# A four-layer graph kernel on one core: the first stage with adjacency products ahead and its loop term on VectorE

## The reference, cut to what matters

```python
# layer 0
msg_in   = (adj   @ x + bias_in ) * sigmoid(x @ gate_w_in  + gate_b_in )
msg_out  = (adj   @ x + bias_out) * sigmoid(x @ gate_w_out + gate_b_out)
msg_loop = x * sigmoid(x @ loop_gate)
y = layernorm(relu(msg_in + msg_out + msg_loop) + x)
# layer 1, its first half
A = adj + I;  dinv = rsqrt(rowsum + colsum - diagonal of A);  A_hat = dinv A dinv
h = relu(batchnorm((A_hat @ y) @ W1.T))          # statistics over all graphs
```

## Time and profile before

| what | value |
|---|---|
| median of 3 runs | 675.87 us (675.26 to 676.02) |
| the profiled execution, its own time | 676.43 us |
| its span in the trace | 674.3 us |
| TensorE busy, matmul / weight load | 634.5 us (94%) / 437.9 us (65%) |
| VectorE busy | 476.5 us (71%) |
| ScalarE busy | 429.0 us (64%) |
| GpSimd busy | 245.8 us (36%) |
| granted TensorE clock, mean | 0.991 of full speed |

### The profile page before, as it was taken

The page is one execution under the profiler, slowest core; times in us unless marked ns, Lnnn a source line. Parts: engine busy times, 40 slices in busy tenths (PEclk is TensorE's granted clock), DMA queues, the critical chain, the costliest instruction groups (busy, mean ns, idle before and its releaser), DMA issues.

```text
span 674.3 us, 9326 instructions
## 1 busy us (share of the span) xinstructions
PE 634.5 (94%) x2698; PEld 437.9 (65%) x2698; DVE 476.5 (71%) x1566; ACT 429.0 (64%) x955; POOL 245.8 (36%) x262
## 2 busy tenths in 40 slices
PE   8899989997799999999999999999999999999993
PEld 6655746545685587577657756765785686577573
DVE  4988886677886757876886787688758766465355
ACT  2766866774946675676668576666847666547562
POOL 4698983003654032324505332431433243002031
PEclk9989999999999999999999999999999999999997
DMA  9224100000000000000000000000000000000000
GB/s 341 95 81 157 44 1 0 1 0 1 0 1 1 0 1 2 0 1 32 1 1 1 32 1 1 32 1 0 2 31 1 0 33 1 0 2 32 1 28 35
DMA packets 4227, 16.83 MB, mean 25 GB/s; under 512 B 464, under 2 KB 464, under 8 KB 4048
## 3 DMA queue, kind: packets, MB, share of 16 engines
q1 hardware_dynamic: 4176, 16.23, 6.3%
HBM read 12.03 MB, written 4.19 MB: 24 GB/s over the span
## 4 chain that ended last, share of the span: by engine, by line
PE 59%; DVE 13%; ACT 7%; issue 3%; POOL 1%; DVEq 0%; ACTq 0%; POOLq 0%
PE QQ L795 21%; PE QQ L807 14%; PE QQ L646 4%; PE PA L750 4%; PE PA L778 3%; PE PB L769 2%; DVE HB L1387 2%; DVE HT L1472 2%; ACT HB L1024 2%; ACT raw L1061 2%; DVE raw L1494 1%; PE PB L731 1%; ACT raw L1073 1%; PE PB L817 1%; PE PA L731 1%
## 5 line engine op out<-in xcount | busy, mean ns | idle before, releaser
L1061 ACT ACTIVATE raw<-QQ,BL 128x256 f32<-128x256 f32 (+4 forms) x312 | 166.8, 558 | 95.6 <-PE QQ L807 52.0
L795 PE MATMUL QQ<-HT,WT 128*128 128x256 f32 (+2 forms) x624 | 205.5, 473 | 6.3 <-ACT raw L1061 3.4
L795 PEld LDWEIGHTS QQ<-HT,WT 128*128 128x128 f32 x624 | 115.8, 190 | 73.1 <-issue 32.1
L396 POOL TENSOR_TENSOR RSD<-VAR,pw 128x8 f32<-128x8 f32 (+1 forms) x42 | 61.8, 1470 | 230.1 <-DVE VAR L1246 230.1
L807 PE MATMUL QQ<-HB,WT 128*128 128x256 f32 (+2 forms) x384 | 114.5, 441 | 1.7 <-DVE HB L1512 1.4
L807 PEld LDWEIGHTS QQ<-HB,WT 128*128 128x128 f32 x384 | 70.1, 190 | 35.9 <-issue 15.3
L510 POOL TENSOR_TENSOR HB<-HB 128x512 f32<-128x512 f32 x28 | 35.2, 1276 | 132.4 <-ACT HB L1014 132.4
L1073 ACT ACTIVATE raw<-raw 128x256 f32<-128x256 f32 (+4 forms) x88 | 41.5, 472 | 39.7 <-DVE raw L1494 31.5
L1484 DVE SCALAR_TENSOR_TENSOR raw<-raw 128x512 f32<-128x512 f32 (+2 forms) x66 | 39.1, 593 | 30.7 <-ACT raw L1061 30.0
L917 ACT ACTIVATE X<-Z,OFF,RSD 128x128 f32<-128x128 f32 x88 | 35.1, 482 | 8.7 <-POOL OFF L402 8.7
L1512 DVE SCALAR_TENSOR_TENSOR HB<-raw 128x256 f32<-128x256 f32 (+4 forms) x48 | 21.9, 457 | 23.2 <-ACT raw L1073 23.2
(11 more groups left out here) (216 smaller groups left out, 1127.4 us busy)
## 6 DMA issues: line engine op xcount, KB each, us to landing
raw<-in_xt SPq DMA_DIRECT2D x8, 512.0 KB, 7.0
four<-in_x SPq DMA_DIRECT2D x8, 512.0 KB, 5.5
out<-four SPq DMA_DIRECT2D x7, 512.0 KB, 2.7
WT<-in_lstm SPq DMA_DIRECT2D x1, 2048.0 KB, 9.5
later<-in_later SPq DMA_DIRECT2D x1, 725.5 KB, 10.3
AD<-in_adj SPq DMA_DIRECT2D x1, 512.0 KB, 6.6
out<-four SPq DMA_DIRECT2D x2, 256.0 KB, 2.1
early<-in_early SPq DMA_DIRECT2D x1, 274.0 KB, 2.9
```

The lines of the kernel that those rows point to most:

```text
L396: pool.tensor_tensor(RSD[kk][:, ts], VAR[kk][:, ts], pw[:, ts], ALU.pow).then_inc(ln[k]["rstd"], some)
L795: mm = pe.matmul(steps_view(Q[q], k), WT[:, 0, (p - 1) * 4 + q, :], ht_view(par, k), start=True, stop=(s == 0))
L1061: act.activation(TG[q][:, at:n], Q[q][:, at:n], ACT.Tanh, scale=0.5 if q == G else 0.25, bias=BL[:, p - 1, q:q + 1]).then_inc(g_ok, 1)
```

## The change

- SP loads the transposed adjacency and x(0) first, then early, xt(0), the plain adjacency, x(1), xt(1), x(2), xt(2), later, xt(3), x(3). The two adjacency matrices have a semaphore each. The diagonal of adj comes ready from the host with early.
- TensorE starts with neighbours(0), then gates(0), neighbours(1), gates(1), neighbours(2), the transposes, gates(2). neighbours(1) writes into other PSUM (`near`), so that it need not wait for mix(0). In the loop, neighbours(g+1) stands behind spread(g-1) and gates(g+2) and ahead of widen(g-1). The warm-up products before the first and the last hop go; row sums and score vectors move behind the stage, where six warm-up products stay of twelve.
- VectorE adds the loop term: eight tiles z = x * gate_loop + z after the mix. hidden_stats comes two groups behind instead of one.
- GpSimd has no loop term. Second bias and sum of both biases are done in halves of 512 columns, and `rstd` of a group stands behind the next group's sum.
- ScalarE computes the first bias for all groups, behind norm_apply and the evacuations, instead of the loop term; it also makes the second scaling of A_hat.

The diff, cut:

```diff
-            sp.dma_start(early[:], early_in).then_inc(early_ok, 16)
-            load_xt(0)
-            sp.dma_start(AD[:], adj).then_inc(adj_in, 16)
-            load_x(0)
+            sp.dma_start(AD[:, 1], adj[:, 1]).then_inc(adjt_in, 16)
+            load_x(0)
+            sp.dma_start(early[:], early_in).then_inc(early_ok, 16)
+            load_xt(0)
+            sp.dma_start(AD[:, 0], adj[:, 0]).then_inc(adj_in, 16)
...
+            def second(g):
+
+                pool.wait_ge(gate_g, g + 1)
+                reach(pool, mix2, min(g - 1, APART))
+                reach(pool, both_ok, NC * (g - 1 - APART))
+                for c in range(NC):
+                    pool.tensor_tensor(by_tile(V2[g % 2][:])[:, c:c + 1], wide(1)[:, c:c + 1], gate(g, 1)[:, c:c + 1],
+                                       ALU.mult).then_inc(second_ok, 1)
             def both_biases(g):
+                for c in range(NC):
+                    s = slice(c * GB * P, (c + 1) * GB * P)
+                    pool.wait_ge(first_ok, TILES * g + GB * (c + 1))
+                    pool.wait_ge(second_ok, NC * g + c + 1)
+                    pool.tensor_tensor(V[g % 2][:, s], V[g % 2][:, s], V2[g % 2][:, s], ALU.add).then_inc(both_ok, 1)
...
-            for g in range(2, GROUPS):
-                if g + 1 < GROUPS:
-                    biases(g + 1)
-                    both_biases(g + 1)
-                rstd(0, g % 2, g)
-                if g + 1 < GROUPS:
-                    with_loop(g + 1)
+            for g in range(APART, GROUPS + 1):
+                if g < GROUPS:
+                    second(g)
+                    both_biases(g)
+                rstd(0, (g - 1) % 2, g - 1)
...
             for g in range(1, GROUPS + 1):
-                if 1 < g < GROUPS:
-                    neighbours(g)
                 spread(g - 1)
                 if g + 2 < GROUPS:
                     gates(g + 2)
+                if 2 < g + 1 < GROUPS:
+                    neighbours(g + 1)
                 widen(g - 1)
...
             squash(2)
+            first_bias(2)
             for g in range(1, GROUPS + 1):
-                if g + 1 < GROUPS:
-                    loops(g + 1)
                 hidden(g - 1)
                 if g + 2 < GROUPS:
                     squash(g + 2)
+                widened(g - 1, (0, 1))
                 norm_apply(0, g % 2, ZS[g % 2], g, X1[:, g]) if g < GROUPS else None
+                widened(g - 1, (2, 3))
+                if g + 2 < GROUPS:
+                    first_bias(g + 2)
...
+                for t in range(TILES):
+                    dve.scalar_tensor_tensor(out=nth(z, t), in0=nth(XIN[:, g % NX], t), scalar=GG[g % 2][:, t, 2:3],
+                                             in1=nth(z, t), op0=ALU.mult, op1=ALU.add).then_inc(loop_ok, 1)
...
             for g in range(GROUPS):
                 mix(g)
-                if g == 0:
-                    setup_late()
-                elif g + 2 < GROUPS:
+                if 3 <= g + 2 < GROUPS:
                     gate_sum(g + 2)
+                if g >= 2:
+                    hidden_stats(g - 2, range(4))
+                if 3 <= g + 2 < GROUPS:
                     gate_out(g + 2)
-                if g >= 1:
-                    hidden_stats(g - 1, range(4))
             setup_last()
+            hidden_stats(GROUPS - 2, range(4))
```

More of the change, by code:

```diff
@@ L163, in build @@
         GBI = first("GBI")
+        DG = first("DG")
         BIO = first("BIO").rearrange("p (k c d) -> p k c d", k=2, c=NC)
@@ L330, in nth, with near @@
             return buf[:, t * P:(t + 1) * P]
+        def near(g):
+            return QA if g == 1 else PB
         def upto(n):
             return min(n, GROUPS)
+        APART = 2
         def slots(slot):
@@ L553, in row_sums @@
                 for m in range(NC):
-                    pe.matmul(Q[1][:, 0:NODES], ones[:], ADJT[:, m, :], start=(m == 0), stop=(m == NC - 1))
+                    pe.matmul(Q[3][:, 2 * P:2 * P + NODES], ones[:], ADJT[:, m, :], start=(m == 0), stop=(m == NC - 1))
             def turn_adj():
@@ L565, in vectors @@
             def vectors():
-                pe.wait_ge(later_ok, 16)
-                pe.matmul(Q[2][:, 0:P + 1], WTR, AR[:, P - 1:2 * P], start=True, stop=True).then_inc(setup_pe, 1)
+                for k in range(2):
+                    pe.matmul(Q[3][:, k * P:(k + 1) * P], AR[:, k * P:(k + 1) * P], WTR, start=True, stop=True)
+                pe.matmul(PB[:, 0:P + 1], WTR, AR[:, P - 1:2 * P], start=True, stop=True).then_inc(setup_pe, 1)
             def gates(g):
@@ L629, in _ @@
                     gates(g + 2)
+                if 2 < g + 1 < GROUPS:
+                    neighbours(g + 1)
                 widen(g - 1)
             pe.wait_ge(gate_z, GROUPS)
-            for k in range(2):
-                mm = pe.matmul(Q[3][:, k * P:(k + 1) * P], AR[:, k * P:(k + 1) * P], WTR, start=True, stop=True)
-            spin(Q[3][:, 2 * P:3 * P], 12)
+            row_sums()
+            vectors()
+            spin(PA[:, 0:P], 6)
             pe.wait_ge(hid_ok, 4 * GROUPS)
@@ L953, in hidden, with widened @@
                     for q in range(2):
+                        act.wait_ge(agg1_ps, 2 * g + q + 1)
                         act.activation(AG[:, q * BANK:(q + 1) * BANK], PA[:, q * BANK:(q + 1) * BANK], ACT.Copy).then_inc(agg1_ok, 1)
[L955 removed]
+            def widened(g, some):
+                for r in some:
+                    q, h = pieces(g)[r]
                     n = 4 * g + r
@@ L965, in _ @@
             first_bias(1)
-            loops(1, loop1_ok)
+            act.wait_ge(setup_pe, 1)
+            for c in range(NC):
+                act.activation(AHT[:, c, :], PA[:, c * NODES:(c + 1) * NODES], ACT.Copy, scale=dinv[:, c:c + 1]).then_inc(turned_ok, 1)
+            norm_apply(0, 0, ZS[0], 0, X1[:, 0])
             squash(2)
-            norm_apply(0, 0, ZS[0], 0, X1[:, 0])
+            first_bias(2)
             for g in range(1, GROUPS + 1):
-                if g + 1 < GROUPS:
-                    loops(g + 1)
                 hidden(g - 1)
```

181 lines of the change are left out of this document (69 added, 112 removed).

## The result

The changed kernel takes 673.11 us, the median of 14 runs (671.33 to 675.06); the kernel before, timed beside it, 676.12 (14 runs, 673.99 to 678.58). The ratio is 0.9956, with a 95% interval of 0.9944 to 0.9968: about 3.0 us faster where 6.4 was forecast. The direction is right, and the size less than half. The times of the changed kernel also scatter over nearly 4 us. How large the gain is, is thus known only roughly; that it is less than half of the forecast holds both times.

A forecast was written before the change was run, and what follows sets the result against it. TensorE's 12.12 us a group tied with a VectorE and GpSimd loop of 12.13. Gains of 1.1 us at the start and 5.3 in the last three groups made 6.4: 670.0 from the profile, 669.5 from the median, range 667.5 to 671.

The forecast's parts named there:

- The steady part: Full groups of the first stage: TensorE's 12.12 us stays the period, with VectorE at 10.7 us a group.
- The cover of 2.2 us on the chain of GpSimd: Per group, the chain from norm_apply through GpSimd's half sums, power and offset takes 9.9 us against 12.12, so is hidden.
- The loop tiles: VectorE's eight added loop-term instructions: 0.205 us each, 1.64 a group, between bounds of 0.15 and 0.27 each.
- The start: From the loads to spread(1): it begins at 41.0 us instead of 42.12, a gain of 1.1 us.
- rival 2: Start and clock give back half: slow spread(1) costs 1.7 us, gates(0) 1.6, up to 3.3; 671 to 673; chance 0.22.
- Is group 7 ready? ... Yes, by 0.8: End of the first stage: mix(7) and its chain finish at 106.8 us, TensorE comes to it at 107.6.
- Rival 3: No change: last groups stay on VectorE's pace, only 1.1 us comes, 674.8; at most 3 x 0.3 lost; chance 0.07.
- The warm-up products ... go ... nothing: TensorE: dropping four warm-up products before the first hop and eight before the last costs nothing.
- The later stages keep their order and get nothing: Stages behind the first: order unchanged, no gain there; the whole 6.4 us comes from the first stage.
- Rival 1: Slower: GpSimd's halves hold VectorE's loop tiles; 680 us at three of four halves, 687 at all four; chance 0.11.

The follow-up runs named there:

- e3, e4: A follow-up run; the text does not tie this label to a particular change and gives no time under it.
- e15: Changed kernel with warm-up products at the start alone (ten before neighbours(0), sixteen behind gates(2), four before spread(1)), a single execution: 676.56 us.
- the first experiment: Changed kernel with the eight warm-up products put back before the last hop, two sessions: 674.34 us, ratio 0.9958, and 672.95 us, ratio 0.9953, to the kernel before.
- the fourth: Kernel before the change, without its eight warm-up products ahead of the last hop: 678.42 us, ratio 1.0024.
- e14: Changed kernel with warm-up products at the start alone (ten before neighbours(0), sixteen behind gates(2), four before spread(1)), a single execution: 673.95 us.
- e7: The changed kernel itself, unedited, run once more for a further profile: 676.33 us.
- e8: The changed kernel itself, unedited, run a third time for a further profile: 672.35 us.
- e11: Changed kernel with neighbours(g+1) behind widen(g-1) and ScalarE's squash behind the first two evacuations: 684.27 us, ratio 1.0128 to the kernel before.

## Why the prediction came out as it did, step by step

**The steady part: right.** The period is 12.17 us for 12.12, TensorE is busy 36.00 of 36. The ReLU, 2.42 us beside GpSimd in the earlier trace rows, takes 1.22. The cover of 2.2 us on the chain of GpSimd held. VectorE is busy 34.65 of 36 us, 11.7 a group instead of 10.7; this did not matter here, as long as it stayed below 12.17.

**The loop tiles: within the bounds, at their upper end.** 0.27 us each (2.19 a group), the price of the mix form; 0.205 was taken "as the nearest row". The statistics read one operand, this form three, and the form counted more than the memory that it reads. It is 0.55 us a group.

**The start: right in sum, by other terms.** spread(1) came at 39.37, forecast 41.0. neighbours(0) took 3.67 and ended at 9.12 instead of 10.9; in two of the other three profiles of this kernel it took 5.79 and 5.91, close to the forecast's 6.0, and spread(1) came at 42.3 and 41.7. From the end of neighbours(0) to spread(1) it is 30.2 us in all four, 30.1 in the forecast. spread(0) ran at half speed (6.03 us) and cost nothing, as rival 2 said of it; its slow spread(1) was seen in two profiles, e3 and e4 (5.38 us both), and half of it in e15 (4.51). What the forecast didn't have is that the first product takes 3.67 in two and 5.8 to 5.9 us in two of the four profiles, and that x(0) lets it start at 5.45 to 6.29 us and not at 4.91. Together with the hop at spread(7) this could make 0.9956 once and 0.9981 another time of the same kernel; how often each value comes up was not counted, so this is argued and not shown.

**"Is group 7 ready? ... Yes, by 0.8": the step that failed.** It counted mix(7) from the end of neighbours(7) and asked VectorE for nothing else. In the profile mix(7) starts 2.75 us after that end: hidden_stats(4), 2.46 us, is ahead of it, and the queue was 1.08 us late from one small sum held beside GpSimd. mix(7)'s own chain to spread(7) took 11.38 us instead of 10.4, of which 0.55 are the loop tiles. Together 3.73 us; 0.54 of them were to spare, and the pause is 3.19. TensorE came to spread(7) at 106.1, as it should, and had to wait. The 2.75 us are made up so: mix(6) already started 1.47 us after its product had ended (86.26 for 84.79), VectorE then needed 11.67 us to mix(7), and the two products end 10.39 apart. The prediction's own terms give 10.1 for that stretch (10.7 less 0.6 for gates, of which group 7 needs none), just below TensorE's 10.4; the loop tiles (0.55) and the held small sum (1.08) took it above. Rival 3 compared 10.7 with 10.4, took 0.3 a group, and did not ask where in the queue mix(7) stands. Moving hidden_stats(4) took 2.26 us of the pause away and 3.7 us of the stretch to the last end, which shows this step; the 0.93 us of pause that stayed are those of the longer chain and of the 0.49 us that mix(7) still came late.

**"The warm-up products ... go ... nothing": the second step that failed.** Behind the pause of 3.19 us the granted clock falls to 0.50 in three of four profiles of the changed kernel, and the hop takes 5.38 instead of 3.69. Leaving the products out cost 1.5 us in those executions, by the first experiment, and 1.7 in the kernel before, by the rows of the fourth. It would indeed be nothing if the pause had not come: with the statistics moved, the hop is at 3.69 without them. So the one error made the other: 26.0 us were forecast from spread(5) to the last end and 30.2 measured, of which 0.3 lie ahead of spread(6), 2.85 between spread(6) and spread(7), and 1.0 in the last hop and its copy.

**"The later stages keep their order and get nothing": almost.** The last widen ends 3.74 us earlier, the span only by 3.0. In this profile 0.54 of the 0.7 that go are lost at one instruction, VectorE's small product (L1387 after the change) in the attention layer, with GpSimd's 512-column one (L491) beside it:

```profile
175.81 1.28 DVE L1387 SCALAR_TENSOR_TENSOR EB<-four,MM 128x4 f32<-128x4 f32 x1
...
175.80 1.27 POOL L491 TENSOR_TENSOR HB<-HB 128x512 f32<-128x512 f32 x1 [0.32 <-ACT HB L997]
```

Before, the same pair began at 179.49 on VectorE and at 179.50 on GpSimd, and the small one took 0.16. TensorE's offset to the kernel before goes from -3.7 to -3.16 us right behind it. This is the rule of the Trainium skill, SBUF — State Buffer, "Who interferes with whom" (a VectorE instruction with two SBUF inputs and a GpSimd one that reads SBUF exclude each other, and the order of issue decides who stands); the trace agrees, here as at the small sum of 1.26 us. But it is not an effect of the change. In the eighteen profiles of all versions the small product is held six times (1.28) and free twelve times (0.16), in the changed kernel two and two, and the two always start within 10 ns of each other. Held, VectorE's started 7 or 8 ns behind GpSimd's; free, from 5 ns ahead to 5 ns behind (the traces hold nanoseconds, the rows round them to ten). So in e14 it starts one step of the rows later and is free:

```profile
176.28 1.30 POOL L491 TENSOR_TENSOR HB<-HB 128x512 f32<-128x512 f32 x1 [0.32 <-ACT HB L1000]
176.29 0.16 DVE L1390 SCALAR_TENSOR_TENSOR EB<-four,MM 128x4 f32<-128x4 f32 x1
```

Nor does it explain the loss: in e7 and e8, where it is free, 553.3 and 553.4 us lie behind the last widen, in the first profile, where it is held, 553.1, and in the kernel before 552.3 (552.6 in e5, its version without the warm-up). So the later stages give back 0.7 to 1.0 us against the one profile of the kernel before in every profile of the changed kernel, whether the small product is held or not, and where is open.

**The rivals.** Rival 1, the lock that makes it slower, did not happen in the steady part: of four halves a group, one meets an instruction of VectorE, and it is the small sum (1.27, 0.91, 1.28 and 1.26 us in four periods), never a loop tile. Ahead of the steady part it did hold one: a loop tile of group 2 takes 1.17 us instead of 0.27 (the eight 3.01 from 39.30), without a cost on TensorE. Its mechanism is real, and it took part in the pause. Rival 2's sizes (1.7 us for a hop at half speed) were right and its place wrong: it looked at spread(1), and the hop that fell was spread(7), where the change had removed the very products that the kernel before kept for it. That 673.11 lies within 0.2 us of its "671 to 673" is luck: the loss has its size and not its cause. Rival 3 is the nearest to what happened, in that the last groups went at VectorE's pace, but it had no cost beyond 0.3 a group and no clock.

Open: what decides an execution's clock at neighbours(0), at spread(1) and at the hop behind the pause; the rest of e11's circle; and the 0.7 to 1.0 us given back in the later stages.

## What to carry to other kernels

When a period gets shorter on one engine, write down the whole queue of each other engine up to the instruction that the last group needs, with every instruction that stands ahead of it, and not only the chain of data; where a stage ends, move ahead what the last group waits for and put the statistics behind. Price a removed warm-up by the pause that would be there if the forecast is late by a few microseconds, not by the pause that the forecast has. And where a product's clock differs between executions of one program, compare the same stretch within traces besides the medians, and in more than one trace of each: neighbours(7) to the last end is 26.64 in three profiles of the changed kernel and 25.14 in the fourth, and 25.15 and 25.14 with the warm-up. One pair of profiles could have shown a gain of 1.5 us or none.

## What was not expected of the hardware

- Behind the same pause of 3.19 us in the same program the granted clock stayed at 1.00 in one execution and fell to 0.50 in another, for 3.69 or 5.38 us of the same sixteen products (6.71 once, with the start warmed). It fell behind a pause of 2.28 us as well (the kernel before without warm-up), and not behind one of 0.93 us, each seen in one profile.
- The first product of the changed order, with eight warm-up products ahead, took 3.67 to 3.94 us in five profiles and 5.76 to 5.97 in five others; with ten, 3.67 in five and 4.09 in one.
- A scalar_tensor_tensor of 128 columns with a scalar from memory takes 0.27 us from tile to tile, whether its first tensor lies in PSUM (2.16 for eight) or in SBUF (2.19).
- A VectorE instruction of 4 or 16 columns with two inputs in SBUF waits for the end of a 512-column instruction of GpSimd that is already running (1.28 and 1.26 us instead of 0.16 and 0.18). For the one with 4 columns, a start 7 ns behind GpSimd's was late enough to be held, and one 5 ns behind was not.
